# Eight-core sandwich block: norm tiles taken twelve ahead, one staging ring of six, halved Q/K products, and the down matrix loaded in twelve pieces

## The reference, cut to what matters

```python
x = x + LN(attn0(LN(x)))   # 16 x 2048 x 1024 f32; S_ = tril(Q K^T)/32, softmax over all columns; out = V * rowsum(A)
x = x + LN(ffn0(LN(x)))    # xr, xk: mixes of x and x shifted by one row; sigmoid(xr Wr) * (relu(xk Wk)^2 Wv)
x = x + LN(attn1(LN(x)))   # 16 heads of 64, full softmax; gelu(A) @ Wpost, plus its own input
x = x + LN(ffn1(LN(x)))    # silu(x wg) * (x wu), hidden 3072, then wd; integer weights times 1/127
```

## Time and profile before

| what | value |
|---|---|
| median of 3 runs | 3344.2 us |
| the runs | 3342.32, 3344.20, 3690.52 us |
| the profiled execution, its own time | 3361.03 us |
| its span, first to last instruction of its slowest core (core 1) | 3360.0 us |
| spans of the 8 cores in it | 3318.4 to 3360.0 us |
| busy: PE, ACT, DVE, POOL | 3110.6, 1853.1, 1565.3, 667.9 us |

### The profile page before, as it was taken

One profiled execution on the slowest core, in us unless ns is written; L12 is line 12 of the kernel. 1 busy time (PEld: TensorE's weight loads), 2 busy tenths in 40 slices (PEclk: granted clock), 3 DMA queues, 4 the chain that ended last, 5 costly groups with the idle time before them and its releaser, 6 DMA issues.

```text
span 3360.0 us, 54664 instructions; the slowest of 8 cores (3318.4 to 3360.0 us)
## 1 busy us (share of the span) xinstructions
PE 3110.6 (93%) x19462; PEld 1222.3 (36%) x19462; DVE 1565.3 (47%) x2808; ACT 1853.1 (55%) x1948; POOL 667.9 (20%) x1157
## 2 busy tenths in 40 slices
PE   6899898999999988669999999999999999999998
PEld 2444443444444432223333333333333333333333
DVE  2456676655565534344344354354354344444431
ACT  2344433333333337776676776776776776776511
POOL 1244535322223220020030030030120120110301
PEclk9899998999999999889999999999999999999987
DMA  7244648344444431663344353354253344343332
GB/s 169 82 151 132 176 113 188 99 127 108 118 132 107 105 104 63 152 151 124 124 135 136 107 155 123 106 162 131 92 162 131 106 148 132 118 136 116 103 122 69
DMA packets 226906, 421.44 MB, mean 125 GB/s; under 512 B 84048, under 2 KB 108624, under 8 KB 225488
## 3 DMA queue, kind: packets, MB, share of 16 engines
q1 hardware_dynamic: 213936, 378.10, 35.5%
q0 software_dynamic: 12704, 39.85, 7.5%
HBM read 357.06 MB, written 104.86 MB: 137 GB/s over the span
## 4 chain that ended last, share of the span: by engine, by line
PE 73%; DVE 8%; ACT 7%; issue 5%; DMA 4%; POOL 2%; SPq 0%; DVEq 0%; POOLq 0%; ACTq 0%; another core or an unknown queue 0%
PE ps L1373 11%; PE ps L1385 11%; PE ps L763 9%; PE ps L1421 9%; PE ps L756 7%; PE p_t L1190 7%; PE ps L1172 6%; ACT c_pt L95 5%; PE p_n L1197 4%; PE ps L520 3%; PE ps L366 2%; PE ps L1316 2%; PE p_n L461 1%; DMA c_v<-s_v 1%; PE p_t L209 1%
## 5 line engine op out<-in xcount | busy, mean ns | idle before, releaser
L95 ACT ACTIVATE c_pt<-ps,negm 128x1024 bf16<-128x1024 f32 x1024 | 1075.3, 1114 | 224.0 <-PE ps L1174 222.9
L1172 PE MATMUL ps<-c_q,c_k 64*128 64x512 bf16 x1024 | 330.4, 386 | 95.8 <-ACT c_pt L95 80.7
L1373 PE MATMUL ps<-c_h,c_wg 128*128 128x512 bf16 x1536 | 375.8, 389 | 16.7 <-DMA c_h<-c_h 16.7
L1385 PE MATMUL ps<-c_h,c_wu 128*128 128x512 bf16 x1536 | 372.8, 387 | 0.0
L1421 PE MATMUL ps<-c_wd,c_hh 128*128 128x512 bf16 x1536 | 363.3, 391 | 5.5 <-DVE c_o L1322 3.2
L1174 PE MATMUL ps<-c_q,c_k 64*128 64x512 bf16 x1024 | 332.8, 388 | 0.0
L1190 PE MATMUL p_t<-c_pt,c_v 128*64 128x512 bf16 x2048 | 323.6, 396 | 1.4 <-DVE c_pvs L1208 1.1
L1379 DVE SCALAR_TENSOR_TENSOR c_th<-c_th,ps 128x512 f32<-128x512 f32 x192 | 132.0, 688 | 400.6 <-ACT c_th L95 400.6
L151 POOL TENSOR_SCALAR c_pof<-c_pof 128x1 f32<-128x1 f32 x32 | 6.6, 206 | 1377.5 <-DVE c_pof L144 1377.5
L95 ACT ACTIVATE c_th<-ps 128x512 f32<-128x512 f32 x192 | 114.7, 597 | 296.5 <-PE ps L1373 274.8
L1391 DVE TENSOR_TENSOR c_hh<-c_th,ps 128x512 bf16<-128x512 f32 x192 | 131.0, 682 | 217.5 <-PE ps L1385 215.9
(11 more groups left out here) (201 smaller groups left out, 4365.5 us busy)
## 6 DMA issues: line engine op xcount, KB each, us to landing
c_wg<-s_wg SPq DMA_DIRECT2D x192, 256.0 KB, 2.7
c_wu<-s_wu SPq DMA_DIRECT2D x192, 256.0 KB, 3.0
s_x<-r_xt SPq DMA_DIRECT2D x64, 512.0 KB, 3.8
c_k<-s_k SPq DMA_DIRECT2D x64, 512.0 KB, 4.8
c_v<-s_v SPq DMA_DIRECT2D x64, 512.0 KB, 5.9
r_xa<-x SPq DMA_DIRECT2D x32, 512.0 KB, 5.2
r_xt<-x SPq DMA_DIRECT2D x32, 512.0 KB, 4.1
r_xa<-s_x SPq DMA_DIRECT2D x32, 512.0 KB, 4.8
```

The lines of the kernel that those rows point to most:

```text
L95: return self.ACT.inc(self.nc.scalar.activation(*a, **k))
L1172: nc.tensor.matmul(bank[:, 0:512], k_[0:64, tc * 128:(tc + 1) * 128], q_[0:64, :], start=True, stop=True, tile_position=(0, 0))
L1373: ins = nc.tensor.matmul(pA, self.wg[j][:, dc * 128:(dc + 1) * 128], self.h3[:, dc * TG:(dc + 1) * TG], start=(dc == 0), stop=(dc == DC - 1))
L1385: ins = nc.tensor.matmul(pB, self.wu[j][:, dc * 128:(dc + 1) * 128], self.h3[:, dc * TG:(dc + 1) * TG], start=(dc == 0), stop=(dc == DC - 1))
```

## The change

1. `prep` of tiles 8 to 11 is emitted inside the 16 groups that make M (after groups 0, 4, 8 and 12), and each of these groups now advances the model clock. A tile step prepares tile T + 12, so that steps 20 to 23 prepare nothing.
2. The two `vs` tiles become numbers 4 and 5 of `t2`; V, Q, K and keys take turns in one ring of six (the first eight takes still use four).
3. In solo mode `two` calls `self.between()` after its first half: two attention steps. After the product three steps follow in place of five.
4. The down matrix is loaded in twelve pieces of 2 rows of blocks at model times 45, 54, ... 144 after `start()`, in place of six pieces of 4 at once.

```diff
@@ phase_a1, the groups of M
                 ev[b] = DVE.inc(v.tensor_copy(dst, src))
+            if n % 4 == 0:
+                prep(8 + n // 4)
             n += 1
+            B.tick(8 * U)
@@ tile_step
-        if T + 8 < 32:
-            prep(T + 8)
-        elif T < 26:
+        if T + 12 < 32:
+            prep(T + 12)
+        elif 24 <= T < 26:
@@ PhaseA2
-        self.t2 = [B.sb(f"b_t{i}", D, BF16) for i in range(4)]
+        self.t2 = [B.sb(f"b_t{i}", D, BF16) for i in range(4)] + vs
@@ t2_take
-        k = self.t2_n % 4
+        n = self.t2_n
         self.t2_n += 1
+        k = n % 4 if n < 8 else (n - 8) % 6
@@ two
             if h == 0:
                 B.tick(8 * U)
+                if self.solo:
+                    self.between()
@@ v_tile
-        vs = self.vs[T % 2]
-        B.ACT.wait(t, self.vs_free[T % 2])
+        k = self.t2_take()
+        vs = self.t2[k]
+        B.ACT.wait(t, *self.t2_free[k])
@@ run, last group
                 self.solo = True
+                self.between = lambda: PB.steps(2)
                 PB.steps(1)
                 for k in range(8):
                     self.qk(7, k < 4, k % 4)
-                    PB.steps(5)
+                    PB.steps(3)
@@ start
-        for c in range(6):
-            dst, o = (self.wd[0], c * 4 * D) if c < 4 else (self.wd[1], (c - 4) * 4 * D)
-            self.t_wd = B.slot("dWd").dma(g.dma_start(out=dst[:, o: o + 4 * D],
-                                                      in_=W["f1_wd"][:, c * 4 * D:(c + 1) * 4 * D]))
+        def wd_piece(c):
+            dst, o = (self.wd[0], c * 2 * D) if c < 8 else (self.wd[1], (c - 8) * 2 * D)
+            self.t_wd = B.slot("dWd").dma(g.dma_start(out=dst[:, o: o + 2 * D],
+                                                      in_=W["f1_wd"][:, c * 2 * D:(c + 1) * 2 * D]))
+
+        for c in range(12):
+            B.after(45.0 + 9.0 * c, lambda c=c: wd_piece(c))
```

More of the change, by code:

```diff
@@ L642, in __init__ @@
         self.th = B.sb("b_th", D, F32)
-        self.vs = [B.sb(f"b_vs{i}", D, BF16) for i in range(2)]
+        vs = [B.sb(f"b_vs{i}", D, BF16) for i in range(2)]
         self.post = Norm(B, "b_post", 4.0 * EPS)
@@ L659, in __init__ @@
         self.w_tok = {}
-        self.t2_free = [[] for _ in range(4)]
+        self.t2_free = [[] for _ in range(6)]
         self.t2_n = 0
@@ L672, in __init__ @@
         self.th_free = None
-        self.vs_free = [None, None]
         self.x2_tok = {}
@@ L892, in v_tile @@
         B.SP.wait(ta)
-        self.vs_free[T % 2] = B.kvq_tok[(s, "v", i_)] = B.slot(f"dVs{T % 2}").dma(B.nc.sync.dma_start(
+        B.kvq_tok[(s, "v", i_)] = B.slot(f"dQs{k}").dma(B.nc.sync.dma_start(
             out=self.SCR["v"][s].rearrange("c p (t e) -> p c t e", e=128)[:, :, i_, :],
             in_=vs[:].rearrange("p (c e) -> p c e", e=128)))
+        self.t2_free[k] = [B.kvq_tok[(s, "v", i_)]]
         B.tick(8 * U)
```

## The result

The changed kernel takes 3360.4 us (median of 5 runs, 3359.4 to 3363.3) against 3344.2: the ratio is 1.0055, with a 95% interval from 1.0041 to 1.0068. It is slower by some 18 us, where 11 us faster had been forecast. Ratios leave out executions of a second, slower state of the chip, medians don't. The experiments ran apart from this result, together with the kernel before, so that ratios to it are given for them; their intervals are wider, from 15 to 41 us from end to end.

What follows compares the result with a forecast made beforehand. PE was taken as the bound nearly everywhere, with gains only in its gaps and the half clock behind them. Terms -7.7 + 0 + 7 - 12.9 + 2.5 = -11.1 us took the median 3344.2 to 3333, range 3312 to 3353.

Steps and rivals of the forecast that it cites:

- Down matrix in pieces: Loads after `start()`: without the burst, -12.9 us; the twelve spread pieces cost waits on the projection's transfers, +2.5 us.
- The prediction's own sign of being wrong: Forecast wrong if PE's reduction wait is missing or over 2.6 us, or `c_x` and `c_h` waits grow over 5 together.
- the spreading only moves the stall: Rival: pieces cost the projection's chain what the burst cost attention, +13 in place of +2.5, total 3344 us; chance 0.14.
- the price by megabytes: Twelve down-matrix pieces of 0.52 MB: each takes 3.1 us of all DMA engines.
- The stall for `c_v`: Attention after `start()`: PE's 11.6 us wait for the v tile goes, with 1.3 us of lower clock after it: -12.9.
- Solo halves: Solo products: halves gain 0.16 us each, but wait 1.3 us for the column sums' reduction; seven boundaries, +7 us.
- Tiles twelve ahead: First stage: PE's waits for `r_h` in steps 20 to 22 and the lower clock behind them go, -7.7 us.
- the early steps: Gaps of steps 1 to 3 taken to stay, 0 us; the rival that they profit too, 14 us, 3319, chance 0.12.
- One ring: Second stage's staging tiles: nothing waits for a free one, so 0 us, from -3 to +3.
- The slower rival: Solo products: the reduction before each half meets DVE busy, starting 3 us later; price 29 us, 3355 us; chance 0.14.

Runs made afterwards that it cites:

- e3: The changed kernel with the six down-matrix pieces issued at once, as in the kernel before; ratio 0.9971 to the kernel before.
- e1: The changed kernel, with every down-matrix piece waiting at its place until PE has got as far as the program had; ratio 0.9955 to the kernel before.
- e9: As e4, with the first held down-matrix piece at model time 88 in place of 45, behind the projection; ratio 0.9897 to the kernel before.
- e4: As e1, with the column sums in solo mode placed at 4.0 in place of 5.0 model us; ratio 0.9909 to the kernel before.
- e12: As e9, with whole solo products, five steps behind each, and the column sums at 5.0 model us; ratio 0.9890 to the kernel before.
- e5: The kernel before with only the tiles prepared twelve ahead; ratio 0.9936 to the kernel before.
- e10: As e9, with V in its own ring of two and a ring of four for the rest; ratio 0.9920 to the kernel before.
- e11: As e9, with six down-matrix pieces of twice the size, 18 model us apart; ratio 0.9893 to the kernel before.

## Why the prediction was wrong

- **Down matrix in pieces, the step that failed.** The prediction said that the pieces come back as "the others about 9.7 us apart until 1567", each worth 0 to 3.1 us in front of a transfer on the path, and took +2.5 (bounds 0 to +8). That took the planner's model time for time on the chip. The text had read what GpSimd does at that place (it foresaw four pieces between steps of the norm chain; there were three), but not what it waits for: from the fourth tile's norm on, nothing. The twelve issues lie within 46 us, not 110. The term measured +35.7 (56.5 in e3 to 92.2), far outside its bounds; with the pieces held it is 7.0 (e1) or 0.3 (e9), inside them. The prediction's own sign of being wrong came true: the waits for `c_x` and `c_h` were to grow by at most 5 us together and went from 5.57 and 5.01 to 8.8 and 43.3. The rival "the spreading only moves the stall" had the right shape, but priced at +13 for the same reason. Nine pieces of 3.1 us are 28 us, so that even the price by megabytes would have been short of the 36. Two x tiles, a store and two transposes shared the engines with the pieces; how the other 8 us come about is open.
- **The stall for `c_v`.** Right: -12.9 forecast, 207.6 (e3) to 196.1 measured, -11.5.
- **Solo halves.** Right in mechanism and size: +7 forecast, +6.8 measured; PE's wait 0.95 us seven times, ACT's gaps 1.67 and 2.89 against 1.6 and near 3. e4 and e12 show the two parts of it: the wait, 7.7 us, and next to nothing from the halves.
- **Tiles twelve ahead.** Right in place, small in size: -7.7 forecast, -11.5 measured by the last mark (e5), from one execution each. The gaps of steps 20 to 22 went, M's groups took the transposes without a wait, and the early steps stayed. The rest of the gain, about 2 us in the first stage and 2 more in the second, wasn't followed to a row.
- **One ring.** 0 forecast; -3.6 by the marks of e9 and e10, not settled.
- **The slower rival** put the loss on the reduction meeting a busy DVE, with 3 us more per boundary. Its seven waits were 6.6 us together on core 5 and 8.1 on core 0, the longest 1.0 and 1.2, so DVE's other work hardly met it. The kernel did become slower, by another mechanism.

Sum of the measured terms: -11.5 + 6.8 - 11.5 + 35.7 = 19.5 us; the timed difference is 18, that of the last marks 21. Spans of cores within one execution differ by more than what is left.

## What to carry to other kernels

A due time in a planner that orders instructions is a place in the order, not a time: a transfer "later" on a queue is later only if something in that engine's stream waits. Before a burst is spread, list what the issuing engine waits for between the pieces, and give each a wait on the bound engine's progress if there is nothing. Price a burst by what is issued behind it, or just before it, and how much cover that has, not by its own length; and when a piece of work moves to just in front of the next user of its buffer, its latency is on the path again.

## What the runs showed of the hardware that was not expected

- The same burst of nine casting transfers delays what shares the engines with it unequally. An x tile of 512 KB, issued 1.4 us before the last transpose, landed after 22.3 us; the transpose (one 128x1024 bf16 tile, 256 KB, 3.1 us before) after 41.35. The other cores agree: 17.4 to 21.9 us for that x tile, 32.5 to 37.8 for the transpose, of half the bytes. That it was the second of two transposes under way may be part of it; no run here separates that.
- Being issued first didn't save a transpose: the one 0.15 us ahead of the burst took 16.2 to 24.3 us.
- Twelve transfers of half a megabyte and six of a megabyte, with the same spacing of the bytes, take the same time within 0.2 us on the stretch where they fall. That doesn't show that a transfer has no fixed cost. On core 0 the median piece of half a megabyte landed after 6.7 us (e9) and that of a megabyte after 10.8 (e11), less than twice as long; but nobody waits for a single piece here, so that such a part costs nothing.
- While nothing ran on PE from 1490 to 1530 us its granted clock fell to 0.50, the lower of its two levels (1.2 GHz against 2.4; the first ten us have a mean of 0.59). The first gate product after it took 3.57 us in place of the 1.83 of the second. It took 3.57 us as well behind the wait of 5.01 us in the kernel before: the 38 us more of standing still cost nothing further in that product.
